# Four-attention block: in the second and third attention, sums beside the products, one reciprocal for 8 heads, one exp over two score banks, steps in another order

## The reference

```python
x = _L0_xattn_ref(x, ctx, ...)    # x 128x256, heads of 64, 256 queries x 256 keys; then a layer norm
x = _L1_xattn_ref(ctx, x, ...)    # 128 queries (latents), 256 keys = context + latents, heads of 16; MLP
x = _L2_xattn_ref(x, ctx, ...)    # layer norm, 128 queries, 128 keys, heads of 16; layer norm, MLP
x = _L3_xattn_ref(x, mask, ctx, ...)  # heads of 8: mean and std of v under the softmax, instance norm
# second and third:
attn = softmax(where(mask, q @ k.T * scale, -big))     # per head
out  = (attn @ v).reshape(rows, 256) @ out_w + out_b + residual
```

## Time and profile before

| | us |
|---|---|
| median of 3 runs (lowest, highest) | 1221.82 (1220.92, 1226.72) |
| the profiled execution | 1221.06 |
| its span, first to last instruction | 1219.3 |
| TensorE busy | 991.2 |
| VectorE busy | 615.7 |
| ScalarE busy | 463.1 |
| GpSimd busy | 267.1 |

### The profile page before, as it was taken

How to read it: one execution, slowest core, us unless ns; L and a number is a source line. 1 busy time by engine, 2 the same in 40 slices (tenths; PEclk the granted TensorE clock), 3 DMA queues, 4 the chain that set the end, 5 groups by cost and what they waited for, 6 DMA issues and landing times.

```text
span 1219.3 us, 20340 instructions
## 1 busy us (share of the span) xinstructions
PE 991.2 (81%) x7888; PEld 612.9 (50%) x7888; DVE 615.7 (50%) x1263; ACT 463.1 (38%) x881; POOL 267.1 (22%) x386
## 2 busy tenths in 40 slices
PE   7888789897897878888798878979788887976672
PEld 6465444564454654555546644546535454444430
DVE  1444544555546654465455555465544555554431
ACT  1414244343442444344342424424343344422223
POOL 0311111142111510232111421115112231023103
PEclk9899999999999999999999999999989999998667
DMA  9200120010200111002200102001020012001001
GB/s 379 93 1 1 70 95 26 6 70 5 96 31 1 74 51 55 22 2 74 95 19 14 66 10 95 31 2 74 9 87 31 2 74 86 17 16 69 5 1 35
DMA packets 29054, 60.60 MB, mean 50 GB/s; under 512 B 9376, under 2 KB 21024, under 8 KB 24096
## 3 DMA queue, kind: packets, MB, share of 16 engines
q1 hardware_dynamic: 28960, 59.29, 13.3%
HBM read 54.04 MB, written 5.24 MB: 49 GB/s over the span
## 4 chain that ended last, share of the span: by engine, by line
PE 68%; DVE 21%; issue 7%; ACT 2%; POOL 1%; DMA 1%; DVEq 0%; SPq 0%; POOLq 0%; ACTq 0%
DVE nm L1358 7%; PE GP L956 5%; PE PV L702 5%; PE GP L564 5%; PE GP L965 5%; PE GP L566 5%; DVE U L1423 5%; PE SC L685 3%; PE SC L771 3%; PE GP L938 3%; PE GP L749 3%; PE GP L788 3%; PE SC L873 2%; PE MX L618 2%; PE GP L948 2%
## 5 line engine op out<-in xcount | busy, mean ns | idle before, releaser
L1358 DVE TENSOR_REDUCE nm<-MX 128x2 bf16<-128x512 f32 (+1 forms) x352 | 227.1, 689 | 203.1 <-PE MX L624 111.5
L1672 POOL TENSOR_TENSOR Psum<-Pr 128x512 f32<-128x512 f32 x56 | 70.9, 1266 | 294.4 <-ACT Pr L1164 294.4
L1166 ACT ACTIVATE Pr<-SC,bcol 128x512 f32<-128x512 f32 x128 | 81.1, 684 | 131.5 <-PE SC L771 131.5
L564 PE MATMUL GP<-zP,W 128*128 128x128 f32 x512 | 103.2, 284 | 6.9 <-DMA W<-w 6.9
L1191 ACT ACTIVATE Pr<-SC,bcol 128x512 f32<-128x512 f32 x96 | 60.8, 684 | 115.8 <-PE SC L873 115.8
L566 PE MATMUL GP<-uP,W 128*128 128x128 f32 x512 | 100.1, 277 | 0.0
L1164 ACT ACTIVATE Pr<-SC 128x512 f32<-128x512 f32 x128 | 69.3, 593 | 62.8 <-PE SC L685 62.8
L564 PEld LDWEIGHTS GP<-zP,W 128*128 128x128 f32 x512 | 79.8, 194 | 15.8 <-issue 13.6
L1646 POOL TENSOR_TENSOR stat<-stat,half 128x1 f32<-128x1 f32 x24 | 13.6, 565 | 326.9 <-DVE stat L1532 179.2
L566 PEld LDWEIGHTS GP<-uP,W 128*128 128x128 f32 x512 | 78.9, 195 | 0.0
L702 PE MATMUL PV<-Pr,V 128*64 128x256 f32 x512 | 75.6, 420 | 0.0
(11 more groups left out here) (184 smaller groups left out, 1709.0 us busy)
## 6 DMA issues: line engine op xcount, KB each, us to landing
WA<-w1a SPq DMA_DIRECT2D x8, 1024.0 KB, 6.0
WB<-w1b SPq DMA_DIRECT2D x8, 1024.0 KB, 8.1
WA<-w2a SPq DMA_DIRECT2D x8, 1024.0 KB, 5.0
WB<-w2b SPq DMA_DIRECT2D x8, 1024.0 KB, 7.1
W<-w SPq DMA_DIRECT2D x6, 1024.0 KB, 9.9
scratch<-U SPq DMA_DIRECT2D x16, 256.0 KB, 2.0
C<-scratch SPq DMA_DIRECT2D x96, 32.0 KB
zP<-z_in SPq DMA_DIRECT2D x8, 128.0 KB, 4.3
```

The source lines that it names most:

```text
L564: pe.matmul(dst, W0[:, piece, 2 * s, at:at + P], zP[:, s * P:s * P + P], start=True, stop=False)
L1166: act.activation(Pr[:, (n + j) % 4, :], SC[j], ACT.Exp, bias=bcol[:, 3 + k % 2:4 + k % 2], scale=8.0 ** -0.5).then_inc(p_ready, 1)
L1358: dve.tensor_reduce(dst, MX[(n + i) % 2][:].rearrange("p (a k) -> p a k", a=a), AX_X, ALU.max, negate=True).then_inc(mx_done, 1)
L1672: pool.tensor_tensor(Psum[:, c % 4, :].rearrange("p (a l) -> p a l", l=D), two[:, :, 0:D], two[:, :, D:2 * D], ALU.add)\
```

## The change

In the second and third attention:

- The value columns of two heads, one of SC[0]'s and one of SC[1]'s, share 32 columns: each head's weights have 16 columns of values and 16 zeros, and both accumulate into the same 32 rows of PSUM. For each product a second one with 16 columns of ones (`ones2`) accumulates the sums at columns 128 to 255 of the same bank. A bank so holds 8 heads and their sums, and there are two banks, two quotients (reciprocal straight from PSUM, no shuffle) and two output matmuls in each attention. The weights of values and output are permuted on the host, the output weights without padding.
- ScalarE takes the exp of both banks with one instruction of 1024 columns.
- TensorE's order: latents and v1c come after the first maxima unit, qp0 after the second; vp0 after all products of the second attention; k3 after the first scores of the third; the transposition (0, 1, "T") and scores0(2) ahead of the output projection. VectorE and ScalarE follow; VectorE does end3 ahead of qp1's addition.
- The mixed schedule: the fourth attention's entry units stand in rows (0, 4) and (0, 5), which come before (3, 0); VectorE's reciprocal of the first attention's sums moves to row (3, 1). In the last batch the entry is as before.
- V3 has a buffer of its own instead of V1's.

```diff
 BOTH = [(0, 0, [], []), (0, 1, [], []), (0, 2, [], []), (0, 3, [], []),
-        (0, 4, [], []), (3, 0, [], [(3, 1, 0)]), (3, 1, [], [(3, 1, 2)]), (0, 5, [(3, 1, "T")], [(0, 3, 0)]),
-        (3, 2, [], [(0, 3, 2)]), (3, 3, [(0, 3, "T")], [(3, 2, 0)]), (0, 6, [], [(3, 2, 2)]),
...
+        (0, 4, [(3, 0, 0)], [(3, 0, 2)]), (0, 5, [(3, 0, "T")], [(3, 1, 0)]), (3, 0, [], [(3, 1, 2)]),
+        (3, 1, [(3, 1, "T")], [(0, 3, 0)]), (3, 2, [], [(0, 3, 2)]), (3, 3, [(0, 3, "T")], [(3, 2, 0)]),
...
                 def pv(c, kc):
                     n = SC_AT[b, L, 2 * (halves * c + kc)]
+                    bank = pv_bank(b, L, c)
+                    if kc == 0:
+                        pe.wait_ge(*pv_bank_taken(b, L, c))
                     for r in range(2):
-                        g = 2 * c + r
-                        bank = pv_bank(b, L, g)
                         pe.wait_ge(p_ready, n + r + 1)
-                        if kc == 0:
-                            pe.wait_ge(*pv_bank_taken(b, L, g))
-                        for t in range(4):
-                            mm = pe.matmul(bank[32 * t:32 * t + 32, 0:P], V(HG * g + t, kc),
-                                           Pr[:, (n + r) % 4, t * P:t * P + P], start=(kc == 0),
-                                           stop=(kc == halves - 1), skip_group_check=True)
+                        for at, weights in ((0, lambda t: V(2 * c + r, t, kc)), (P, lambda t: ones2[:, r, :])):
+                            for t in range(4):
+                                mm = pe.matmul(bank[32 * t:32 * t + 32, at:at + P], weights(t),
+                                               Pr[:, (n + r) % 4, t * P:t * P + P], start=(at == kc == r == 0),
+                                               stop=(kc == halves - 1 and r == 1), skip_group_check=True)
                         mm.then_inc(pv_done, 1)
...
-                    for s in range(NG):
-                        if s == 2 and between:
-                            between()
-                        pe.wait_ge(s_Ax, 8 * b + 4 * which + s + 1)
+                    for s in range(2):
+                        pe.wait_ge(s_Ax, 4 * b + 2 * which + s + 1)
...
+                    if (g, u) == (0, 0):
...
+                        v1("v1c", 0)
+                    if (g, u) == (0, 2):
+                        fill("qp0")
...
+                attention12(b, 1, make, K1, lambda g, t, kc: V1[:, kc, slot(g, t):slot(g, t) + 32],
+                            (s_V1, 2 * b + 2), amid1, after=after1)
+                fill("vp0")
                 slots_out("o1", W1O, 0)
...
+                def before2(i):
+                    if i == 0:
+                        g, full = begin("k3", (ld_w3, 16))
+                        pe.matmul(g[:, 0:D], W3[:, 1, :], uC[:], start=True, stop=True).then_inc(full, 1)
...
+                    if more:
+                        make03[0](1, "T" if i else 2)
...
+                if more:
+                    scores0(b + 1, 2)
+                slots_out("o2", W2O, 1)
...
             def attention12(b, L, scale, after=lambda i: None):
-                for i in range(8 if L == 1 else 4):
...
+                for i in range(4 if L == 1 else 2):
+                    n = SC_AT[b, L, 2 * i]
+                    act.wait_ge(sc_full, n + 2)
+                    pr_taken(act, n + 1, 1)
+                    bias = bcol[:, i % 2:i % 2 + 1] if L == 1 else bcol[:, 2:3]
+                    act.activation(Pr[:, n % 4:n % 4 + 2, :], SCP[:], ACT.Exp, bias=bias, scale=scale)\
+                        .then_inc(p_ready, 2)
+                    after(2 * i + 1)
...
-                    if L == 0 and k == 5:
+                    if (L, k) == ((0, 5) if b < 0 else (3, 1)) and b < B - 1:
                         reciprocals0(b + 1, 0)
...
-            def quotient(b, L, g):
+            def quotient(b, L, m):
...
-                chain.step(dve.stream_shuffle(den, bank, [16 + r % 16 for r in range(32)]))
-                chain.step(dve.reciprocal(den, den))
-                dve.tensor_tensor(Ax[:, g, :], bank, den, ALU.mult).then_inc(s_Ax, 1)
+                chain.step(dve.reciprocal(den, bank[:, P:2 * P]))
+                dve.tensor_tensor(Ax[:, m, :], bank[:, 0:P], den, ALU.mult).then_inc(s_Ax, 1)
...
+                attention12(b, 1, amid1)
+                if not is_first(b):
+                    end3(b - 1)
+                fill("qp1")
+                quotient(b, 1, 0)
+                if more:
+                    maxima(b + 1, 0, 0, 0)
+                    maxima(b + 1, 0, 0, 2)
+                quotient(b, 1, 1)
...
+                attention12(b, 2)
+                if more:
+                    maxima(b + 1, 0, 1, 2)
+                quotient(b, 2, 0)
+                if more:
+                    maxima(b + 1, 0, 1, "T")
+                quotient(b, 2, 1)
```

More of the change, by code:

```diff
@@ L98, in mix @@
             if (L, k) == (3, 0):
-                units(b, ENTRY)
+                units(b, entry(b))
             units(b, middle)
@@ L808, in mixed @@
                     if (L, k) == (3, 0):
-                        for name in ENTRY:
+                        for name in entry(b):
                             unit(*name)
@@ L852, in mix_end, with attention12 @@
                     project("kp0", order_of(b + 1), b + 2)
[L854 removed]
+            def attention12(b, L, make, K, V, v_ready, amid=lambda g, u: None, before=lambda i: None,
+                            after=lambda i: None):
                 halves = 2 if L == 1 else 1
@@ L898, in attention12 @@
                     scores(c, kc)
+                    before(i)
                     if i == 1:
                         pe.wait_ge(*v_ready)
-                    for _, g, u in (then[i] if i < len(then) else []):
+                    for _, g, u in (units[cuts[i]:cuts[i + 1]] if i + 1 < len(cuts) else []):
                         make(g, u)
@@ L985, in body, with amid1 @@
                 v1("v1", 1)
-                def amid1():
-                    wait(pe, *pv_bank_taken(b, "lat"))
-                    for c in range(2):
-                        mm = pe.transpose(pv_bank(b, "lat")[:, c * P:c * P + P], hT[:, c, P:D], ident[:])
-                    mm.then_inc(s_latT, 1)
-                    v1("v1c", 0)
-                    fill("qp0")
+                def amid1(g, u):
+                    if (g, u) == (0, 0):
+                        wait(pe, *pv_bank_taken(b, "lat"))
+                        for c in range(2):
+                            mm = pe.transpose(pv_bank(b, "lat")[:, c * P:c * P + P], hT[:, c, P:D], ident[:])
+                        mm.then_inc(s_latT, 1)
+                        v1("v1c", 0)
+                    if (g, u) == (0, 2):
+                        fill("qp0")
                 make = maxima_pass(b, 1, K1b, b1row[:],
@@ L1386, in mix_end, with attention12 @@
                     quotient0(b + 1, 3)
-            def attention12(b, L, amid=lambda: None, after=lambda: None, during=lambda g: None):
-                units = UNITS1 if L == 1 else UNITS2
-                for _, g, u in units:
-                    if (g, u) == (0, "T"):
-                        amid()
+            def attention12(b, L, amid=lambda g, u: None):
+                for _, g, u in UNITS1 if L == 1 else UNITS2:
                     maxima(b, L, g, u)
-                after()
-                for g in range(NG):
-                    quotient(b, L, g)
-                    during(g)
+                    amid(g, u)
             def reciprocals0(b, half):
@@ L1519, in body, with amid1 @@
                 more = not is_last(b)
-                def after1():
-                    fill("qp1")
-                    if not is_first(b):
-                        end3(b - 1)
-                attention12(b, 1, lambda: (v1("v1c", 0), fill("qp0")), after1,
-                            lambda g: maxima(b + 1, 0, 0, 2 * g) if more and g < 2 else None)
+                def amid1(g, u):
+                    if (g, u) == (0, 0):
+                        v1("v1c", 0)
+                    if (g, u) == (0, "T"):
+                        fill("qp0")
+                attention12(b, 1, amid1)
+                if not is_first(b):
+                    end3(b - 1)
+                fill("qp1")
+                quotient(b, 1, 0)
[3 more added lines that the diff above has]
+                quotient(b, 1, 1)
                 g = take(o, "o1")
@@ L1551, in body @@
                 blocks12(b, o, 2)
-                attention12(b, 2, after=lambda: maxima(b + 1, 0, 1, 2) if more else None,
-                            during=lambda g: maxima(b + 1, 0, 1, "T") if more and g == 1 else None)
+                attention12(b, 2)
[5 more added lines that the diff above has]
+                quotient(b, 2, 1)
                 g = take(o, "o2")
```

127 lines of the change are left out of this document (62 added, 65 removed), and 4 rows, old and new, of the table BOTH.

## The result

| us | before | after |
|---|---|---|
| median (lowest to highest), 4 runs each | 1223.36 (1220.92 to 1226.72) | 1101.30 (1100.86 to 1102.02) |
| span of the profiled execution | 1219.3 | 1100.2 |
| mean granted clock | 0.947 | 0.970 |

The ratio is 0.9001, 95% interval 0.8976 to 0.9026: faster. The forecast was 1114.7. The profiled execution took 1102.02, 12.7 less than the forecast, which was worked out from the profiled execution of the kernel before. The runs of the kernel before spread from 1220.6 to 1227.5 us over all sets, at mean clocks of 0.947 down to 0.941, and its profiled execution, 1221.06 at 0.947, is of the quick end, so a difference of spans from it can be some 4 us smaller than the difference of medians.

A forecast was written before the change was run, and what follows sets the result against it. TensorE's work, busy 81%, sets most of the time, the rest its waits for VectorE. Seven batches of 4.8 + 5.8 + 4.2 (103.6), less 1.0, plus 3.8, give 106.4: from 1221.06 to 1114.7 us, range 1096 to 1143, chance 0.66.

The forecast's parts named there:

- Quotient, 1.4: Second and third attention: a quotient without shuffle, read from PSUM, takes 1.4 us; two instead of four in each.
- Sums, 1.15 a group: Product groups on TensorE: 32 instructions instead of 16 take 1.15 us instead of 0.57, adding 3.4 us a batch.
- Exp, 1.09, worth 0.2 on the path: ScalarE: one exp of 1024 columns takes 1.09 us, 0.17 less than the pair's 1.27.
- Second attention, 4.8: Second attention, first maxima to xa: moved fills and hidden quotients bring xa at 530.9 instead of 535.72, 4.8 us less.
- Third attention, 5.8: Third attention to xa: fewer quotients and k3 moved earlier bring xa at 573.0 instead of 578.88, 5.8 us less.
- (a): Clock stays low: 1.4 us in the mixed part and about 1.5 in the third attention not won; 1135 us; chance 0.11.
- Mixed schedule, 4.2, of it 1.4 clock: Fourth attention's first maxima: filled waits win 3.5 us and higher clock 1.4, less about 0.7 new rests; 4.2 us less.
- Last batch, 3.8: Last batch: no fills, wins only two quotients in each attention against doubled products, about 2 + 1.8 = 3.8 us.
- (b): VectorE becomes the bound of the second attention; maxima and quotient 1 slip 2 us; 1130 to 1140 us; chance 0.09.
- (c): TensorE's own work is dearer: product groups above 1.15 us, 0.5 each would be 24 us; 1139 us; chance 0.08.
- (d): Slower kernel: more, narrower matmuls replace waits and clock is low through all three stretches; 1353 us; chance 0.02.
- (e): Quotients and moves win only half, other waits taking their place one for one; 1168 us; chance 0.02.

The follow-up runs named there:

- experiment 2: Kernel after with old mixed table, two exps and moved steps put back, leaving packing and V3's own buffer: 1166.79 us, ratio 0.9544.
- experiment 4: Kernel after with each product of the ones (the sums) made a second time: 1114.15 us, ratio 0.9103.
- experiment 6: Kernel after with two exps of 512 columns in place of the one of 1024: 1100.36 us, ratio 0.8974.
- Experiment 8: Kernel after with vp0 put back between the scores of the second attention: 1110.79 us, ratio 0.9061.
- experiment 7: Kernel after with latents, v1c and qp0 put back ahead of the second attention's first transposition: 1108.70 us, ratio 0.9054.
- experiment 9: Kernel after with k3's projection back behind all products of the third attention, its evacuation behind the exps: 1106.78 us, ratio 0.9037.
- experiment 1: Kernel before with only the new table of the mixed schedule: 1194.52 us, ratio 0.977.
- experiment 3: Kernel before with six filler matmuls after each of the fourth attention's first two maxima units: 1217.11 us, ratio 0.9949.
- experiment 10: Kernel after with 5 to 12 filler bf16 matmuls in each of eight TensorE waits of the last batch: 1094.96 us, ratio 0.895.
- experiment 11: Kernel after with last-batch wait fillers, two exps, last batch's latents and v1c put back, fillers in its fourth attention: 1093.76 us, ratio 0.8931.
- experiment 5: Kernel after with the old table of the mixed schedule put back: 1137.60 us, ratio 0.9274.

## Why the prediction was right, and where its numbers were off

The direction, the places and the order of the parts held: the forecast's own case came, with the median 13.4 us below it and inside the range. Two steps failed all the same, the size of the sums and the mechanism of the last batch, and one near hit is in part luck: see the second attention. By its steps:

- **Bound.** Right. The waits for Ax went and 119.1 us of span with them; the stages without such waits moved by 0.1 us at most (xa to x1 15.53 and 15.53, xa to x3 15.99 and 16.09).
- **Quotient, 1.4.** In the third attention it takes 1.35 (518.69 to 520.04). Experiment 2 puts the packing, two quotients for four with the sums against them, at 2.2 us in the second attention and 6.1 in the third, 1.6 of that clock.
- **Sums, 1.15 a group.** This term was mis-sized. The group takes 1.01, and 16 sums more cost 0.44, of which 0.22 to 0.33 reach the end (experiment 4). The row that I scaled, 0.57 for 16, has a fixed part of about 0.13: (1.45 - 1.01) / 16 = 27 ns for each further instruction. I had set the estimate by the Trainium skill (TensorE: Matmul & The Clock Gate, Wait — 56ns, not 53.3ns?), 0.8, aside for the row's 36 ns. The measured 1.01 lies between the two, and the increment of 27 ns is near the floor of about 25 ns that the Trainium skill gives there. The row's mean had the fixed part in it, and the estimate by the floor leaves it out.
- **Exp, 1.09, worth 0.2 on the path.** The size was right (1.11), the 0.2 wrong: experiment 6 shows none. I had named the later first product as its price, and missed two others: the next *scores*, one matmul of which needs only the first bank, and the exp itself, which now waits for both. The estimate of 1.37 for the pair, which I drew from the Trainium skill (Advanced Engine Details and Errata, The Read-Write Bubble), was too high: the pair takes 1.26. That one large instruction is 0.15 shorter than two agrees in direction with the latency between instructions that the Trainium skill tells of there.
- **Second attention, 4.8.** Measured 5.03. That this is so near is in part luck: the sums of its four groups cost 1.33 instead of 2.3 and the exp wins nothing instead of 0.2, which would make it 5.6; the 0.6 that other terms erred the other way, no run separates. The cover of quotient 1 stands as forecast: it ends at 485.02, under vp0, which ends at 485.28. Timeline of the kernel after:

```profile
483.29 1.13 PE L581 MATMUL GP<-W,zP 128*128 128x512 f32 x2
...
483.75 0.95 DVE L1439 RECIPROCAL U<-PV 128x128 f32<-128x128 f32 x1
484.26 1.02 PE L582 MATMUL GP<-W,uP 128*128 128x512 f32 x2
484.73 0.29 DVE L1440 TENSOR_TENSOR Ax<-PV,U 128x128 f32<-128x128 f32 x1
485.12 1.03 PE L958 MATMUL GP<-W1O,Ax 128*128 128x256 f32 x4
```

  Experiment 8 prices that cover at 1.24 and experiment 7 the earlier latents, v1c and qp0 at 1.57.
- **Third attention, 5.8.** Measured 6.8, of it 1.6 clock, where rival (a) had put 1.5. From its first exp to xa I had 573.0 - 564.44 = 8.56 and it is 522.65 - 514.98 = 7.67. The differences: second scores 0.25 earlier (k3's 0.70 fits the wait for the maxima nearly whole), the product group 0.14 shorter, two quotients 0.1 shorter each (1.35 for 1.45), and the rest hand-overs:

```profile
514.80 0.70 PE L1061 MATMUL GP<-uC,W 128*128 128x256 f32 x2
514.98 1.11 ACT L1210 ACTIVATE Pr<-SC,bcol 128x1024 f32<-128x1024 f32 x1 [1.69 <-PE SC L884]
...
515.99 1.01 ACT L1306 ACTIVATE K<-GP,cols,hmask 128x256 f32<-128x256 f32 x2
517.66 1.11 ACT L1210 ACTIVATE Pr<-SC,bcol 128x1024 f32<-128x1024 f32 x1 [0.66 <-issue]
518.69 0.16 DVE L435 TENSOR_TENSOR gate<-half 128x1 f32<-128x1 f32 x1 [0.92 <-issue]
522.65 0.42 DVE L1586 TENSOR_TENSOR xa<-GP,res 128x256 f32<-128x256 f32 x1 [1.15 <-PE GP L958]
```

  k3's evacuation (L1306) ends 0.66 ahead of the second exp; I had 0.7. Moving k3 back costs 0.27 (experiment 9).
- **Mixed schedule, 4.2, of it 1.4 clock.** Measured 4.5 in the mean of the middle batches, and 4.4 in a typical batch of experiment 1, of it 1.6 clock by experiment 3. That the slow product group was slow by its clock is shown. What I had missed is that the low clock can leave one stage and come in another, as it did in experiments 1 to 3: the low clock went from all middle batches only with the table and the packing together.
- **Last batch, 3.8.** Here a step failed: "has no fills and wins only two quotients in each attention". The last batch won 9.6, and not in those places: second attention 0 (forecast 2), third 4.8 (1.8), its MLP 4.0 (nothing), the rest 0.9. k3's projection and the latents move there too, which I didn't count, and the clock, which I had put at nothing there, sets most of it. Moving latents and v1c leaves a wait of 1.56 ahead of the transposition, and the scores behind it take 1.96 instead of 1.09:

```profile
976.75 0.22 PE L670 MATMUL MX<-identb,nm 128*128 128x128 bf16 x1 [1.56 <-DVE nm L1381]
...
978.61 1.96 PE L884 MATMUL SC<-work,K 64*128 64x512 f32 x4
```

  Undone (experiment 7), the stage is 1.3 shorter. The MLP of the last batch, whose work is the same in all kernels but for the fillers of experiments 10 and 11, goes by its clock: 20.24 us at 0.66 before, 16.22 at 0.89 now, 14.77 at 1.00 with the fillers of experiment 10. Its 16 output matmuls took 6.67 us before and take 3.69 now:

```profile
1158.71 6.67 PE L965 MATMUL GP<-WB,work 128*128 128x256 f32 x16 [2.87 <-DVE work L1461]
```

  So these 4.0 us can't be put down to a part of the change. Experiment 3, which leaves the code of the last batch as it was, has 17.56 at 0.81, and so have experiment 2 and, within 0.02, experiments 5, 7 and 9. Small moves of work ahead of the stage shift its low clock; the forecast had no term for that.
- **Sum.** Of the 12.7 us, 9.9 are the seven batches (112.5 measured for 102.6), 5.8 the last one, less 3.0 of a longer start.
- **Rivals.** (a) The clock stays low: no, 1.00 in all three stretches. It does stay low somewhere in every kernel above that lacks the table or the packing: with the old table the mixed stage is at 0.93 to 0.96 and up to 48.9 us long. (b) VectorE bounds the second attention: no, busy 14.43 of 22.5. (c) TensorE dearer: the other way. (d), (e): no.

## What to carry to other kernels

A wait on the busiest engine cost twice here: the wait itself, and then a lower clock in the work behind it. To price it, look for the same instruction group at both levels (1.97 for 1.08), but read the clock of all stages before you book the gain, as it may only move (experiments 1 to 3). Before an instruction is fused over two buffers, ask who waits for the first buffer alone, and whether the instruction itself could have started on it: the saving of 0.15 us was lost there. And a move that fills a wait in the steady state should be looked at again in the last iteration, where its filling isn't there.

## What the runs showed of the hardware that was not expected

- Useless matmuls can pay. Where TensorE waited 1.6 to 3 us for VectorE, 5 to 12 bf16 matmuls of 512 columns into a free bank raised the granted clock of the work behind: in the MLP of the last batch from 0.89 to 1.00, in its stretch before from 0.78 to 0.95. That won 6.3 us in the last batch alone. In the kernel before, six in each of two waits of a batch won 6.5 us of span, less than their stage's 1.6 a batch, as low clock came in other stages. Real work in the same wait is worth more (4.4 a batch against 1.6).
- Parts that touch different stages aren't additive. The same table change was worth 4.5 us to its own stage in one kernel and 4.9 in the other, and in the first it made two unchanged stages up to 0.8 and 1.7 us longer. The granted clock of such a stage is 0.86 where it is 1.7 longer, and 1.00 where it isn't. The last batch's MLP had three lengths with the same work, by its clock: 20.2 at 0.66, 17.6 at 0.81, 16.2 at 0.89.
- Two exps in a row on different banks overlap by about 0.1 (2 x 0.68 against 1.26), in the kernel before and in experiment 6.
- Matmuls of 32 columns of weights cost 27 ns for each further one in a group, 32 ns as the mean of 32, 36 ns as the mean of 16.
